# The table and weight stage of an attention-and-FFN kernel: loads reordered, index, mask and rotary-weight work moved to POOL, the first LayerNorm and query compression put inside the weight turns

## What is computed

```python
kv_c = ctx @ W_kvc                      # ctx: 16 x 361 x 512, kv_c: 128 wide
q_c  = layernorm(x) @ W_dq              # 192 wide
q_nope, q_rope = q_c @ W_uq, rope(q_c @ W_qr)     # 16 heads, 128 and 64 wide
k_nope, v = kv_c @ W_uk, kv_c @ W_uv
k_rope = rope(kv_c @ W_kr)              # one for all heads
scores = (q_nope . k_nope + q_rope . k_rope) / sqrt(192)
# a query sees the keys seg_id-8 .. seg_id only (9 keys at most)
x = x + (softmax(masked scores) @ v) @ W_o
x = x + ffn(layernorm(x))               # silu(gate) * up, then down, 1408 inner
```

## Time and profile before

| | |
|---|---|
| median of 3 runs | 880.51 us (879.74 to 881.12) |
| profiled execution, first to last instruction | 881.7 us |
| of it, the table and weight stage | up to 115.0 us |
| PE busy | 821.4 us, 93% |
| DVE, ACT, POOL busy | 482.7, 423.9, 282.5 us |
| DMA | 68.93 MB, 78 GB/s over the span, 299 GB/s in the turns from 38.5 to 100.5 us |

### The profile page before, as it was taken

The page is one execution under the profiler, slowest core; times in us unless marked ns, Lnnn a source line. Parts: engine busy times, 40 slices in busy tenths (PEclk is TensorE's granted clock), DMA queues, the critical chain, the costliest instruction groups (busy, mean ns, idle before and its releaser), DMA issues.

```text
span 881.7 us, 15762 instructions
## 1 busy us (share of the span) xinstructions
PE 821.4 (93%) x5662; PEld 780.0 (88%) x5662; DVE 482.7 (55%) x986; ACT 423.9 (48%) x979; POOL 282.5 (32%) x433
## 2 busy tenths in 40 slices
PE   4899998999998999989999899987999999999997
PEld 3788788889998899988999889987999999999997
DVE  2887855544665446653466444655459344445342
ACT  3688643554445535444355444555558623223231
POOL 1455668528043371525524173352000000000000
PEclk9899999999999999999999999999999999999999
DMA  9799631022110212002120121103711121111021
GB/s 235 249 312 306 203 99 40 27 48 63 46 29 14 62 49 59 13 13 77 32 59 26 30 57 31 53 28 100 324 31 30 30 61 32 59 30 59 0 76 30
DMA packets 33201, 68.93 MB, mean 78 GB/s; under 512 B 6182, under 2 KB 15414, under 8 KB 33156
## 3 DMA queue, kind: packets, MB, share of 16 engines
q1 hardware_dynamic: 24100, 41.81, 16.4%
q0 software_dynamic: 9056, 26.52, 9.1%
HBM read 57.03 MB, written 11.27 MB: 77 GB/s over the span
## 4 chain that ended last, share of the span: by engine, by line
PE 65%; POOL 7%; issue 5%; ACT 4%; DMA 3%; DVE 2%; POOLq 0%; DVEq 0%; ACTq 0%
PE ps L1245 16%; PE ps L966 16%; PE ps L861 9%; PE ps L1277 8%; PE ps L913 4%; POOL gathered L796 3%; DMA gathered<-kv_table,idx 3%; PE ps L888 3%; PE ps L891 3%; POOL rot_s L815 1%; DVE o_lo L1101 1%; POOL rot L819 1%; PE ps L903 1%; ACT q_lat L1003 1%; ACT o_hi L1011 1%
## 5 line engine op out<-in xcount | busy, mean ns | idle before, releaser
L796 POOL DMA_INDIRECT gathered<-kv_table,idx x120 | 129.0, 1075 | 34.9 <-issue 34.4
L1101 DVE TENSOR_TENSOR o_lo<-q_lat,o_hi 128x320 fp32r<-128x320 f32 x80 | 64.7, 812 | 108.9 <-ACT o_hi L1011 108.9
L966 PE MATMUL ps<-o_hi,wvo_hi 128*128 128x320 f32 x320 | 104.8, 328 | 7.4 <-DVE o_lo L1101 7.2
L1011 ACT ACTIVATE o_hi<-q_lat 128x320 fp32r<-128x320 f32 x80 | 65.4, 823 | 76.3 <-PE ps L966 75.8
L966 PE MATMUL ps<-o_lo,wvo_hi 128*128 128x320 f32 x320 | 99.5, 311 | 0.0
L966 PE MATMUL ps<-o_hi,wvo_lo 128*128 128x320 f32 x320 | 99.4, 311 | 0.0
L888 PE MATMUL ps<-key_latT,q_lat 128*112 128x126 f32 x480 | 92.3, 274 | 0.0
L891 PE MATMUL ps<-key_ropeT,q_rope 128*112 128x126 f32 x480 | 91.9, 273 | 0.0
L1003 ACT ACTIVATE q_lat<-ps 128x224 f32<-128x224 f32 x120 | 42.9, 357 | 83.9 <-PE ps L913 81.4
L966 PEld LDWEIGHTS ps<-o_hi,wvo_hi 128*128 128x128 f32 x320 | 60.7, 190 | 19.7 <-DVE o_lo L1101 19.1
L1329 ACT ACTIVATE silu<-ps,ffn_scale 128x320 f32<-128x320 f32 x55 | 29.0, 527 | 97.5 <-PE ps L1245 97.5
(11 more groups left out here) (175 smaller groups left out, 2044.0 us busy)
## 6 DMA issues: line engine op xcount, KB each, us to landing
ctx_raw<-ctxT_dram SPq DMA_DIRECT2D x16, 722.0 KB, 7.8
head_w<-head_w_dram SPq DMA_DIRECT2D x16, 576.0 KB, 5.1
ffn_raw<-ffn_w_dram POOLq DMA_DIRECT2D x11, 768.0 KB, 11.2
kv_table<-tab POOLq DMA_DIRECT2D x16, 288.0 KB, 6.5
rows<-x_dram SPq DMA_DIRECT2D x5, 640.0 KB, 5.1
residual<-x_dram SPq DMA_DIRECT2D x20, 160.0 KB, 2.3
x_rows<-residual SPq DMA_DIRECT2D x20, 160.0 KB, 2.0
rows<-x_rows SPq DMA_DIRECT2D x5, 640.0 KB, 4.8
```

Source lines behind the costliest of these rows:

```text
L796: pool.indirect_dma_start(out=kvg[:, s % SLOTS, g, :], out_offset=None, in_=table, in_offset=bass.IndirectOffsetOnAxis(ap=idx[:, k:k + 1], ...
L966: last = pe.matmul(ps[:, 4 + m, 0:TB], w[wt][:, h, cols], xs[h % 2][:, :], start=(h == 0 and n == 0), stop=(h == H - 1 and n == 2))
L1011: act.activation(o_hi[h % 2][:, :], q_lat[:, h % 2, :, h // 2], ACT.Copy).then_inc(oh_ok, 1)
L1101: dve.tensor_tensor(o_lo[h % 2][:, :], q_lat[:, h % 2, :, h // 2], o_hi[h % 2][:, :].bitcast(F32), ALU.subtract).then_inc(ol_ok, 1)
```

## The change

In `build_setup`: 8 turns are written out instead of 4 (the loop then has two passes of four). SP's first loads come in another order. POOL's loads of `wdq`, `mask`, `cosq` and `sinq` move into its turns 1, 3, 3 and 5. POOL takes over the rotary weights (`rope_weights`, in each turn, ahead of `rope` of the turn before), the index work (turn 0), the two mask casts (turn 2) and the key masks (turn 6, with a subtraction and a square in place of the comparison for inequality). ACT and DVE lose that work. The fold of the key matrix (L320, L324) goes from ACT to DVE. The first product of a head goes to spare columns of the sequence's own PSUM banks, and ACT copies it ahead of the table's partial sums. That leaves bank 6 for the first block's row transposes, which PE does in turns 4 and 5, and for its two compression products in turns 6 and 7, with the copies on ACT and the low halves on DVE in the same turns; the tail after the last turn and the `split_compressed` of the first block go. `ctx_hi1` no longer lies over the index inputs, and `compress` gets its bank as an argument. The bodies of `index_work` and `mask_work` are left as they were (less the last MEMSET), on `pool` instead of `dve`.

```diff
-def turns(eng, turn, first=0):
-    for n in range(4):
-        turn(n, 0, n)
-    with eng.Fori(1, NB // 4) as q:
+LN_BANK = 6
+def turns(eng, turn):
+    for n in range(8):
+        turn(n, n // 4, n % 4)
...
         sp.dma_start(wkvcT, a["wkvcT"].rearrange("p (c k) -> p c k", c=KC)).then_inc(kr_in, 16)
         sp.dma_start(wkr[:, :], a["wkr"]).then_inc(kr_in, 16)
+        load_ctx(0, 0)
         sp.dma_start(wkv_raw[:, :, 0:KVC], a["wkvc"]).then_inc(w_in, 16)
-        load_ctx(0, 0)
+        load_head(0, 0)
+        load_ctx(1, 1)
         for dst, name in ((segp, "segp"), (segh, "segh"), (base, "row_base"), (joff, "joff"), (joff9, "joff9")):
             sp.dma_start(dst[:, :], a[name]).then_inc(seg_in, 16)
+        sp.dma_start(rows[:, :, :], a["x"][0:TB, :].rearrange("(t p) d -> p t d", p=LT)).then_inc(x_in, 16)
+        load_head(1, 1)
+        load_ctx(2, 2)
         sp.dma_start(other32[:, :], a["other"]).then_inc(mask_in, 16)
         sp.dma_start(blocks32[:, :], a["blocks"]).then_inc(mask_in, 16)
-        load_ctx(1, 1)
-        load_head(0, 0)
-        sp.dma_start(rows[:, :, :], a["x"][0:TB, :].rearrange("(t p) d -> p t d", p=LT)).then_inc(x_in, 16)
-        load_ctx(2, 2)
-        load_head(1, 1)
         load_ctx(3, 3)
...
         pool.dma_start(cosk[:, :, :], a["cosk"]).then_inc(rk_in, 16)
         pool.dma_start(sink[:, :, :], a["sink"]).then_inc(rk_in, 16)
-        pool.dma_start(ident[:, :], a["ident"]).then_inc(const_in, 16)
-        pool.dma_start(w["mask"][:, :], a["mask"]).then_inc(const_in, 16)
-        pool.dma_start(w["cosq"][:, :, :], a["cosq"]).then_inc(const_in, 16)
-        pool.dma_start(w["sinq"][:, :, :], a["sinq"]).then_inc(const_in, 16)
-        pool.dma_start(w["wdq"][:, :, :], a["wdq"]).then_inc(const_in, 16)
-        pool.wait_ge(rk_in, 32)
+        pool.dma_start(ident[:, :], a["ident"]).then_inc(ident_in, 16)
         table_rows = table.rearrange("(b t p) c -> b p t c", t=KT, p=P)
         def rope(n, q, i):
             t = tab[i % 2]
+            if isinstance(n, int) and n == 0:
+                pool.wait_ge(rk_in, 32)
...
+        def rope_weights(n, q, i):
+            def at(name, rows=slice(0, P)):
+                return w[name][rows, bass.ds(n, 1), :].rearrange("p o c -> p (o c)")
+            low = slice(R, P)
+            pool.wait_ge(hw_in[i % 2], 16 * (2 * q + i // 2 + 1))
+            pool.tensor_copy(at("wr_hi"), hw[i % 2][:, QR:QR + R]).then_inc(r_hi, 1)
+            pool.tensor_copy(at("wr_2"), hw[i % 2][:, QR + R:QR + 2 * R]).then_inc(r_hi, 1)
+            pool.wait_ge(r_hi, 2 * n + 2)
+            pool.tensor_tensor(at("wr_lo"), hw[i % 2][:, QR:QR + R], at("wr_hi").bitcast(F32),
+                               ALU.subtract).then_inc(r_lo, 1)
+            pool.wait_ge(r_lo, 2 * n + 1)
+            pool.tensor_tensor(at("wr_2", low), hw[i % 2][low, QR + R:QR + 2 * R],
+                               at("wr_2", low).bitcast(F32), ALU.subtract).then_inc(r_lo, 1)
+            pool.wait_ge(r_lo, 2 * n + 2)
+        done = [0]
+        def link(ins):
+            done[0] += 1
+            ins.then_inc(chain, 1)
+            pool.wait_ge(chain, done[0])
+        def index_work():
+            pool.wait_ge(seg_in, 80)
+            link(pool.tensor_copy(segf[:, :], segp[:, :]))
...
+            link(pool.tensor_copy(w["idx_all"][:, :], key[:, :]))
+        def mask_work():
+            pool.wait_ge(mask_in, 32)
...
+        def key_mask_work():
+            neg = w["neg_all"][:, :].rearrange("p (g j) -> p g j", j=WIN)
+            link(pool.tensor_copy(seghf[:, :], segh[:, :]))
+            link(pool.tensor_tensor(keyh[:, :, :], seghf[:, :].unsqueeze(2).to_broadcast([SR, ALLG, WIN]),
+                                    joff9[:, :].unsqueeze(1).to_broadcast([SR, ALLG, WIN]), ALU.add))
+            link(pool.tensor_scalar(neg, keyh[:, :, :], 0.0, float(LK - 1), ALU.max, ALU.min))
+            link(pool.tensor_tensor(neg, neg, keyh[:, :, :], ALU.subtract))
+            link(pool.tensor_tensor(neg, neg, neg, ALU.mult))
+            link(pool.tensor_scalar(neg, neg, 0.0, NEG, ALU.is_gt, ALU.mult))
+        def turn(n, q, i):
             if isinstance(n, int) and n == 0:
-                ln.root(pool, 0)
-        turns(pool, rope)
+                index_work()
+            rope_weights(n, q, i)
+            if not isinstance(n, int) or n >= 1:
+                rope(n - 1, q, i - 1)
+            if isinstance(n, int):
+                if n == 1:
+                    pool.dma_start(w["wdq"][:, :, :], a["wdq"]).then_inc(wdq_in, 16)
+                if n == 2:
+                    ln.root(pool, 0)
+                    mask_work()
+                if n == 3:
+                    pool.dma_start(w["mask"][:, :], a["mask"]).then_inc(const_in, 16)
+                    pool.dma_start(w["cosq"][:, :, :], a["cosq"]).then_inc(const_in, 16)
+                if n == 5:
+                    pool.dma_start(w["sinq"][:, :, :], a["sinq"]).then_inc(const_in, 16)
+                if n == 6:
+                    key_mask_work()
+        turns(pool, turn)
+        rope(NB - 1, 0, NB - 1)
         for i in range(2):
             pool.wait_ge(tab_out[i], 16 * (NB // 2))
...
         def high_weights(n, i):
-            act.wait_ge(mm, n + 1)
+            act.wait_ge(l_mm, n + 1)
             b = 3 * (i % 2)
-            act.activation(part[i % 2][:, :, :], ps[:, b:b + 3, ROW:2 * ROW], ACT.Copy).then_inc(part_ev, 1)
-            act.wait_ge(l_mm, n + 1)
             for k, name in enumerate(("wl_hi", "wl_2")):
                 act.activation(w[name][:, bass.ds(n, 1), :].rearrange("p o c -> p (o c)"),
-                               ps[:, 6, k * P:(k + 1) * P], ACT.Copy).then_inc(l_hi, 1)
+                               ps[:, b + k, 2 * ROW:2 * ROW + P], ACT.Copy).then_inc(l_hi, 1)
+            act.activation(part[i % 2][:, :, :], ps[:, b:b + 3, ROW:2 * ROW], ACT.Copy).then_inc(part_ev, 1)
...
-            for k, name in enumerate(("wr_hi", "wr_2")):
-                act.activation(w[name][:, bass.ds(n, 1), :].rearrange("p o c -> p (o c)"),
-                               hw[i % 2][:, QR + k * R:QR + (k + 1) * R], ACT.Copy).then_inc(r_hi, 1)
...
         def turn(n, q, i):
-            if isinstance(n, int) and n == 1:
-                act.wait_ge(index_ok, 1)
-                act.activation(hi[1][:, :, LK + 1:TROWS], zero[:, :, :], ACT.Copy)
             high_context(n, q, i)
+            if isinstance(n, int) and n in (4, 5):
+                ln.high(act, 0, 2 * (n - 4), (LN_BANK, LN_BANK))
             if not isinstance(n, int) or n >= 1:
                 high_weights(n - 1, i - 1)
+            if isinstance(n, int) and n in (4, 5):
+                ln.high(act, 0, 2 * (n - 4) + 1, (LN_BANK, LN_BANK))
+            if isinstance(n, int) and n in (6, 7):
+                first_high(n - 6)
         turns(act, turn)
         high_weights(NB - 1, NB - 1)
-        for t in range(NLT):
-            ln.high(act, 0, t, (0, 1))
...
-                index_work()
             if isinstance(n, int):
-                for piece in ((0, 1, 2, 3), (4,), (5,), (6,))[n]:
+                for piece in {1: (0, 1, 2, 3, 4), 3: (5, 6)}.get(n, ()):
                     ln.piece(dve, 0, piece, x_in)
+                if n in (6, 7):
+                    first_low(n - 6)
         turns(dve, turn)
         low_weights(NB - 1, 0, NB - 1)
-        key_mask_work()
...
+        def turn_rows(t):
+            if t:
+                pe.wait_ge(ln.hi_ok, t)
+            ln.turn(pe, 0, t, (LN_BANK, LN_BANK))
         def turn(n, q, i):
             later = not isinstance(n, int)
             b = 3 * (i % 2)
+            if not later and n == 4:
+                pe.wait_ge(ident_in, 16)
+            if not later and n in (4, 5):
+                turn_rows(2 * (n - 4))
+            if not later and n in (6, 7):
+                if n == 6:
+                    pe.wait_ge(wdq_in, 16)
+                else:
+                    pe.wait_ge(qc_lo_ok, 1)
+                compress(pe, 0, n - 6, LN_BANK, w, rowsT, ps, ln, qc_mm)
...
+            if not later and n in (4, 5):
+                turn_rows(2 * (n - 4) + 1)
...
-                last = pe.matmul(ps[:, 6, k * P:(k + 1) * P], hd[:, UQ + k * P:UQ + (k + 1) * P],
+                last = pe.matmul(ps[:, b + k, 2 * ROW:2 * ROW + P], hd[:, UQ + k * P:UQ + (k + 1) * P],
                                  hd[:, UK:UK + P], start=True, stop=True)
...
-        pe.wait_ge(tab_sum, NB - 1)
-        for t in range(NLT):
-            ln.turn(pe, 0, t, (0, 1))
-        for m in range(2):
-            compress(pe, 0, m, w, rowsT, ps, ln, qc_mm)
...
```

More of the change, by code:

```diff
@@ L116, in build @@
         low_flag = sb("low_flag", [1, 1], I32)
-        qc_mm = sem("qc_mm")
+        qc = [sem(name) for name in ("qc_mm", "qc_hi_ok", "qc_lo_ok")]
         ffn = {}
@@ L144, in build @@
             w[name] = sb(name, shape, dt)
-        build_setup(nc, a, w, ps, ident, table, rows, rowsT32, four32, ln_q, qc_mm)
```

(34 more changed lines are left out.)

79 lines of the change are left out of this document (36 added, 43 removed).

## The result

The changed kernel takes 909.61 us (median, 908.75 to 910.97) against 880.82 (879.74 to 881.63) on the same chip: a ratio of 1.0321, 95% interval 1.03 to 1.0341. The profiled execution spans 907.5 us against 881.7. I had forecast 887.1 with a range from 875.5 to 897: the sign was right, the size was not. The shift was +28.8 us instead of +6.6. The two spans differ by 25.8 only: in the changed kernel the device time stands 1.65 us above the span (909.15), so the span before belongs, by this estimate, to an execution of some 883.4 us, above its median.

A forecast was written before the change was run, and what follows sets the result against it. The prediction took POOL's in-order list as the bound: its sum of 118.8 put the seam 6.3 us later, and 880.5 + 6.3 + 0.3 for the clock gave 887.1 us, range 875.5 to 897.

The forecast's parts named there:

- What bounds: At the seam before the attention: the change is worth only the shift of POOL's first MEMSET, forecast +6.3 us.
- The tail: After the last turn: taking transposes and 6.26 us of compression out gives at most 3.1 us.
- The start: First turns: the new load order gains at most the second loading hole, 3.3 us; with the tail 6.4.
- What POOL gets: POOL's in-order list through the stage, summed from instruction prices: 118.8 to the end of the last store's issue.
- the 0.3 for bubbles: Turns 2 and 3: 0.3 us added because head 2 and a table sum arrive only just ahead of POOL.
- Key masks: POOL in turn 6: five instructions and their waits, 11.7 us, range 10.5 to 17.
- Rotary weights: POOL, 16 times: 1.5 us each in written-out turns, 1.7 in the loop, 25.6 in all (21 to 41).
- my dearer rival: Rotary weights in the loop: each computed address costs POOL 0.36 us, 9.9 more, time 897; chance 0.12.
- What the lateness hides: Turns 4 to 7: POOL's lateness covers PE's moved transposes and compression, at most 1.5 + 6.3 us.
- The clock: Start of the query products: half clock after PE's idle time, mostly absorbed by a 2.7 us wait; 0.3 us taken.
- The cheap case: POOL's list: lower-end prices give a sum of 108.9, seam at 111.2, time 877; chance 0.25.
- The third rival: Turns: loading and PE bound them, moved PE work unhidden lengthens four turns by 6.8 us, time 881; chance 0.08.

The follow-up runs named there:

- e7: Changed kernel, rotary weights on ACT and DVE, key masks spread over DVE's turns 3 to 7, POOL's table-store wait just before its first gather; 0.9956 of the kernel before.
- e3: Changed kernel with index work, casts, key masks and rotary weights given back from POOL to ACT and DVE; 880.12 us, 0.9972 of the kernel before.
- e11: e3 with the loads of SP and POOL in the order of the kernel before; 882.12 us, 0.9995 of the kernel before.
- e1: Changed kernel with only the key masks given back to DVE, after its last turn; 895.47 us, 1.0148 of the kernel before.
- e9: e7 with index work and mask casts on DVE too, leaving POOL only rotation and stores; 879.95 us, 0.9986 of the kernel before.
- e12: The kernel of e7 run again on another chip; 878.44 us, 0.9959 of the kernel before.

## Why the prediction was wrong

**What bounds.** Right. The shift of one instant, POOL's first MEMSET, is the change's worth: +26.57 us, where the span grew by 25.8.

**The tail.** Wrong in size. I took the 2.8 us landing of the earlier trace rows as the end of the stage. In every run that kept POOL's wait at the end of the stage, the MEMSET follows the last store's issue by 5.2 us: 136.42 to 141.65, 123.96 to 129.18, 106.81 to 112.02. Only the kernel before had more, 6.1, since there the compression ended later. The shortest landing in a group is not what the next block starts behind, and in e7, without the wait, 4.0 us pass all the same. So the tail could give 115.08 − (108.94 + 5.2) = 0.9 us and not 3.1, and the forecast seam was 2.1 us too early.

**The start.** Right within a microsecond: POOL's index work starts at 14.48 against 14.0. The second hole closed (300 GB/s from 14.5 to 38.5). But of start and tail together e3 shows 3.1 us at the seam (115.08 to 112.02), where I had said 6.4 at best.

**What POOL gets.** This step failed: its sum came to 118.8 for the end of the last store's issue, which was 137.23. The seam missed its forecast, 121.4, by 20.2 us; 18.4 of them are in this sum and 2.1 in the tail, less the 0.3 for bubbles that did not come. By its own terms:

- Index inputs +0.5. Index work 7.2 against 5.4, +1.8, of which 1.4 is one `min` beside a `ctx_lo` (1.90 us where the compares after it take 0.52).
- Stretched instructions in rotation and rotary weights, a term that I did not have: +16.1, the largest. I read the earlier trace rows as POOL's price of a rotation; they were its price at a time when DVE could not be in the way. Once POOL stopped waiting for DVE, its instructions fell anywhere in DVE's turn. With the `min` above and one key-mask product below (+1.3) the stretches come to 18.8 us, as much as the whole miss of the sum. The trace before held one sign of it: the root, 1.39 us at 31.91 beside a `ctx_lo` (30.74 to 32.40), took 1.07 in the changed kernel with no `ctx_lo` beside it.
- Key masks 16.5 against 11.7, +4.8. The TENSOR_SCALARs are +5.7, one stretch +1.3, and the three TENSOR_TENSORs −1.8, nearer the lower slope (2.14, 2.49 and 1.99 undisturbed). I chose the one-input price because one input is read; the other bound, 2.8, would not have held 3.88 either. The Trainium skill, page "GPSIMD Engine Reference", section 4.1, has one-input work at roughly line rate. Multiply-add agrees (0.49 us for 360), min and compare do not (1.12).
- Rotary weights, undisturbed, 8 × 1.27 + 8 × 1.49 = 22.1 against 25.6: −3.5. Their computed addresses cost 0.22 us a turn, near the 0.2 of my sum, so the mechanism of my dearer rival, 1.24 us more, is out.
- Rotation and store undisturbed 3.29 and 3.67, as forecast, and no 0.1 between: −1.5. The casts, the root and the issues: −0.5.

The sum is 17.7 of 18.4. Of the rest, 0.4 is a copy of the rotary weights that took 0.65 us instead of 0.24 (at 123.22, beside a `ctx_lo`), and 0.3 a longer gap before one store (0.98 us instead of 0.67).

**What the lateness hides.** Borne out as far as the runs go: PE waits 26.2 us for DVE behind POOL, room enough for its moved work. But the step that put a price on that work without the cover, 6.8 us, was wrong: e3 and e11 have no cover, and their last stores are at 106.81 and 108.28 against 108.94.

**The clock.** PE had stood idle for 14.61 us, and the query products then ran at half the granted clock (0.51 over 5.8 us, the 1.2 GHz level), as forecast; the first key transpose is 20.57 us behind the seam against 18.08. The 2.7 us wait of the earlier trace rows that was to take it up does not lie at the first transpose (133.16) but at the fourth group of them (145.60), and it shrank to 1.3 us. The span grew by 0.8 us less than the seam, within the spread of what lies behind it, so my 0.3 us is not tested.

**The rivals and the range.** The cheap case needed everything at its lower end. The third rival's mechanism did not show in e11, though e3's 880.12 us lie near its 881. The dearer one gave 897 for a reason that proved false; the time is 12.6 us past it. What lay outside the range was not a bound set too near but a term left out: I priced each instruction of POOL by the rows and never asked what DVE does to it.

## What to carry to other kernels

Before work is put on an engine with idle time, look at when that time is and who would run beside it: POOL's instructions measured behind a wait for DVE were cheap because DVE was elsewhere. An operation never seen on an engine is priced in its own kind (one spare slot of idle time gave seven prices), and a stage's end is read from issue to the next instruction, not from the shortest landing. In the fastest kernels POOL kept what fits in the stretch where it has nothing to do, and was given next to nothing in the turns where its output is waited for.

## What the runs showed of the hardware

- Short POOL instructions that met a DVE TENSOR_TENSOR with two SBUF inputs ended 0.1 to 0.5 us behind it: 0.24 to 0.59 us undisturbed became 0.65 to 1.9, and 2.87 beside DVE's normalisation and `ctx_lo` in a row. DVE pays too: `ctx_lo` has a median of 1669 ns and a maximum of 2994, where it started inside POOL's first long TENSOR_TENSOR with two tensors (L359). With a DVE MEMSET of the same tile the effect is gone; with four pieces it is spread, but twice a product stood through all four.
- Two limits of that. A DVE TENSOR_SCALAR with one input tensor did the same to a POOL product (0.39 us became 0.86, e1). And one long POOL TENSOR_SCALAR (L358, from 66.78) kept its 3.87 us beside a `ctx_lo` that began 0.2 us later; there only DVE was slower, 2.41 us.
- On POOL a TENSOR_SCALAR costs by its operation: 360 elements took 0.49 us in multiply-add, 1.12 in min or compare, 1.45 in two such steps, and 1080 elements 3.88. DVE took 0.22 us at 120 elements for a min, a compare and a multiply-add alike (e9), POOL 0.52 for a compare.
- From the issue of a 288 KB store to the first instruction of the next block passed 5.2 us in ten kernels, and 4.0 in e7, e9 and e12, in which POOL did not wait there for the store. DMA data moved in a small part of it, as these windows of the changed kernel show (last two columns; its store was issued at 136.42):

```profile
137.00:137.50 0.50, 0.00 (x0) 0.00 (x0) 0.00 (x0) 0.00 (x0) 0.23 (x1) 0.50 0.00 0
137.50:138.00 0.50, 0.00 (x0) 0.00 (x0) 0.00 (x0) 0.00 (x0) 0.00 (x0) 0.50 0.43 147
138.00:138.50 0.50, 0.00 (x0) 0.00 (x0) 0.00 (x0) 0.00 (x0) 0.00 (x0) 0.50 1.10 359
138.50:139.00 0.50, 0.00 (x0) 0.00 (x0) 0.00 (x0) 0.00 (x0) 0.00 (x0) 0.50 0.24 83
139.00:139.50 0.50, 0.00 (x0) 0.00 (x0) 0.00 (x0) 0.00 (x0) 0.00 (x0) 0.50 0.00 0
```
